# A two-layer attention and mixture-of-experts kernel: layer 0's experts computed on their chosen tokens only

## The chip, the cores and the metric

The kernel runs on one core of a Trainium2 chip. The metric is the device time of one execution in microseconds (us). Engines are named as the profile names them: PE (TensorE matmuls; PEld its weight loads), DVE (VectorE), ACT (ScalarE), POOL (GpSimd) and SP (SyncE, which only starts DMAs here). Each engine runs its own list of instructions in order, and they wait for each other by semaphores.

## The reference

`x` is 8 tiles of 128 tokens with 512 features. Four residual steps follow one another, each on a layer-normed `x`: attention 0, feed-forward 0, attention 1, feed-forward 1. Only feed-forward 0 is changed:

```
scores = sigmoid(x @ gate_w.T) + bias             # 1024 tokens, 16 experts
topk_w, topk_idx = top_k(scores, 4)
cw = one_hot(topk_idx) * topk_w / sum(topk_w)     # zero for the 12 experts not chosen
g, u = x @ Wg[e].T, x @ Wu[e].T                   # 512 -> 256, for every expert e
out  = sum_e cw[:, e] * ((silu(g) * u) @ Wd[e].T) # 256 -> 512
out += (silu(x @ Sg.T) * (x @ Su.T)) @ Sd.T       # a shared expert, for all tokens
```

## The kernel before

Every product of two matrices is made in three matmuls: each operand is split in a high part (a copy rounded to fp32r, made on ACT) and a low part (the rest, made on DVE or POOL), and `three` gives hi*hi, hi*lo and lo*hi. So each weight that arrives by DMA costs a copy and a subtraction before PE may use it.

Attention 0 ends at 279 us of the span. Then `tensor_experts`, `scalar_experts` and `vector_experts` run over 34 passes: 17 experts (the shared one is number 0), each on two halves of 512 tokens. A pass is 4 groups of 12 matmuls into the hidden layer (`tensor_hidden`, 128 hidden units by 512 tokens each) and 4 groups of 6 out of it (`tensor_output`). Every expert sees every token; `vector_output` adds the result times `cw`, which is zero for most. One expert's weights are 1.5 MB, loaded by SP (`sync_experts`, L859) into one of two buffers, and split in 6 chunks of 128x512 by ACT (L904) and DVE (L909) once per two passes. The routing (`vector_routing`, about 12 small DVE operations) lies beside matmuls of pass 1.

Attention 1 follows. Its start is `opening`: keys of the context half, the layer norm of `x` (norm group 4), keys of the latent half; then `half_steps` with values and queries. In the kernel before, this opening is woven into the last expert passes. `scalar_weight`/`vector_weight` split its weights, 256 KB each, loaded by SP at L1147.

All orders are written out by hand: each engine's list is the order of the calls in its function. POOL does nothing between 279 us and the first softmax of attention 1 (it waits at L1349).

Of the kernel before, what the change touches and what calls it, by code (L numbers as in the profile page):

```python
# [8 lines left out]
U32 = mybir.dt.uint32  # L9
ALU = mybir.AluOpType  # L10
# [3 lines left out]
P = 128  # L14
B = 8
# [13 lines left out]
CH = 512  # L29

# [114 lines left out]
def layers_kernel(nc, A, out):  # L145
    with ExitStack() as whole:
# [66 lines left out]

        place[0] = PHASE
        xnB = pair("xnB", [P, KT, HT])
        xnT = [xnA, xnB]
        s_act = [sb(f"silu{i}", [P, HT]) for i in range(2)]
        z = [sb(f"z{i}", [P, HT]) for i in range(2)]
        zs = [pair("zs0", [P, IT, HT])]
# [7 lines left out]
        cw = sb("cw", [P, B, E0])  # L227
        zs.append(pair("zs1", [P, IT, HT]))
        raw.append(sb("wf_raw1", [P, 3, 2, CH]))
        wf.append(pair("wf1", [P, 3, 2, CH]))  # L230
        above_experts = place[0]
        mx = sb("mxf", [P, B, 8])
# [14 lines left out]
        k1T = pair("k1T", [P, KV1, 2, HT])  # L247
        place[0] = w1_at = max(place[0], above_experts)
# [5 lines left out]
        outw = [pair(f"w1o{i}", [P, D]) for i in range(UH)] + outw  # L254
        mx1 = [sb(f"mx1_{i}", [P, 4 * UH]) for i in range(4)]

# [61 lines left out]

        def norm_scale(g, k):
            t, b = HB * g + k, norm_tile(g, k)  # L320
            if t >= 2:
                dve.wait_ge(S["xn_turned"], t - 1)
            nc.vector.tensor_scalar(xn[t % 2][:, :], x[:, b, :], moments[:, b, 0:1], rstd[:, b:b + 1],  # L323
                                    ALU.subtract, ALU.mult).then_inc(S["xn"], 1)

        def norm_turn(g, k, n):
# [4 lines left out]
            for c in range(KT):  # L331
                ins = nc.tensor.transpose(ps[:, c * P:(c + 1) * P], xn[t % 2][:, c * P:(c + 1) * P], ident)  # L332
# [31 lines left out]
        def sync_attention0():  # L364
# [7 lines left out]
            load(bk[:, :], A["bk0"]).then_inc(S["ld_bk0"], 16)  # L372
# [3 lines left out]
            load(bv[:, :], A["bv0"].broadcast_to([P, P])).then_inc(S["ld_bv0"], 16)  # L376
            load(w_raw[:, :, :], A["wq0"]).then_inc(S["ld_wq0"], 16)
            load(bq[:, :], A["bq0"]).then_inc(S["ld_bq0"], 16)
            load(bo[:, :], A["bo0"].broadcast_to([P, D])).then_inc(S["ld_bo0"], 16)
# [151 lines left out]
        def scalar_attention0():  # L531
            def keys(half):
                act.wait_ge(S["k0_mm"], half + 1)
                act.wait_ge(S["ld_bk0"], 16)
# [30 lines left out]
            def query(half, m):  # L565
                act.wait_ge(S["ld_bq0"], 16)
# [7 lines left out]
            def out_weight(k):  # L574
                act.wait_ge(S["ld_wo0"], 16)
                nc.scalar.activation(wo[0][:, k, :], w_raw[:, k, :], ACT.Copy).then_inc(S["wo0_hi"], 1)
# [1337 lines left out]
```

## Time and profile before

| | us |
|---|---|
| median of 3 runs | 1607.87 (1607.38 to 1609.44) |
| the profiled execution, its own time | 1609.84 |
| its span in the trace | 1608.5 |
| PE busy / DVE / ACT / POOL | 1550.5 / 932.6 / 708.3 / 298.1 |
| DMA queue of SP | 78.03 MB, 14.7% of the 16 engines' time |

PE is busy for 96% of the span. The granted clock of TensorE is 0.978 of full speed on average. The times of single matmuls overlap (each is modelled as 0.39 us long, while one starts every 0.23 us), so the pace of PE is read from starts, or from a run of matmuls divided by its count.

### The profile page before, as it was taken

Reading aid. Unit: us, or ns where it says so; the run is one execution under the profiler, and the core shown is the slowest. Engines: PE = TensorE matmul, PEld = TensorE weight load, DVE = VectorE, ACT = ScalarE, POOL = GpSimd, SP = SyncE. Lnnn points to the kernel's source line nnn. Section 1 sums busy time; section 2 is a strip of 40 time slices with the busy share of each in tenths; the row PEclk is TensorE's granted clock in tenths of the full one; section 3 lists DMA queues with packets and bytes.
Section 4 is the critical chain, followed back from the end, with each engine's and each line's share of the span. In section 5 each row is a group of like instructions: output and inputs, shape, how many; then the busy total and the mean of one; then the engine's idle time right before and its main releaser. Section 6 shows DMA issues by size and latency. Waiting matters only on the chain.

```text
span 1608.5 us, 19926 instructions
## 1 busy us (share of the span) xinstructions
PE 1550.5 (96%) x7394; PEld 1253.3 (78%) x7394; DVE 932.6 (58%) x1762; ACT 708.3 (44%) x1899; POOL 298.1 (19%) x566
## 2 busy tenths in 40 slices
PE   6989988999999999999999999999989999999997
PEld 5667655788888888888887888888877888888875
DVE  5576885545444444444545566666764566666767
ACT  3665875422222222222223455555653455555632
POOL 4354563000000000000000123223220222232200
PEclk7699999999999999999999999999999999999999
DMA  5000100211211112111011211112121121121101
GB/s 187 1 1 1 41 1 10 109 40 40 78 40 40 40 41 77 40 40 59 0 53 31 68 53 58 55 53 66 53 66 53 53 63 62 53 68 58 66 0 53
DMA packets 29666, 79.30 MB, mean 49 GB/s; under 512 B 3969, under 2 KB 4353, under 8 KB 26881
## 3 DMA queue, kind: packets, MB, share of 16 engines
q1 hardware_dynamic: 29568, 78.03, 14.7%
q8 instruction: 58, 0.95, 0.2%
q14 instruction: 40, 0.32, 0.1%
HBM read 75.92 MB, written 2.10 MB: 48 GB/s over the span
## 4 chain that ended last, share of the span: by engine, by line
PE 88%; DVE 6%; ACT 3%; POOL 1%; issue 1%; DMA 1%; SPq 0%; DVEq 0%; ACTq 0%
PE bank L352 75%; PE bank L1381 5%; PE bank L1357 3%; PE bank L490 2%; PE bank L478 2%; ACT p L587 1%; POOL p L817 1%; DVE xn L323 1%; DVE p0T_lo L723 1%; DVE k0d_hi L684 1%; PE bank L332 0%; DVE stats L304 0%; DMA ctx_raw<-in_ctxT 0%; ACT p0T_hi L596 0%; DVE xnA_lo L346 0%
## 5 line engine op out<-in xcount | busy, mean ns | idle before, releaser
L1349 POOL TENSOR_SCALAR p<-p,mx 128x256 f32<-128x256 f32 x256 | 163.8, 658 | 1104.6 <-DVE mx L1343 1104.6
L945 DVE TENSOR_TENSOR z<-bank,silu 128x512 f32<-128x512 f32 x68 | 47.0, 691 | 202.7 <-PE bank L352 201.0
L938 ACT ACTIVATE zs_hi<-z 128x512 fp32r<-128x512 f32 x68 | 43.0, 632 | 188.4 <-DVE z L945 188.4
L1335 ACT ACTIVATE p<-bank,mx 128x256 f32<-128x256 f32 x256 | 118.1, 486 | 11.3 <-DVE mx L1325 11.1
L352 PE MATMUL bank<-xnA_hi,w1q_hi 128*128 128x512 f32 x288 | 117.9, 409 | 2.2 <-DVE xnA_lo L346 1.7
L969 DVE SCALAR_TENSOR_TENSOR x<-bank,cw,x 128x512 f32<-128x512 f32 x128 | 93.8, 748 | 38.0 <-PE bank L352 38.0
L352 PE MATMUL bank<-xnA_hi,w1q_lo 128*128 128x512 f32 x288 | 114.1, 396 | 0.0
L352 PE MATMUL bank<-xnA_lo,w1q_hi 128*128 128x512 f32 x288 | 113.5, 394 | 0.0
L817 POOL TENSOR_SCALAR p<-p,sx 128x128 f32<-128x128 f32 x256 | 91.6, 379 | 113.6 <-DVE sx L711 113.4
L352 PE MATMUL bank<-wf_hi,zs_hi 128*128 128x512 f32 x272 | 108.0, 397 | 1.8 <-DVE zs_lo L948 1.8
L352 PE MATMUL bank<-wf_lo,zs_hi 128*128 128x512 f32 x272 | 107.5, 395 | 0.0
L352 PE MATMUL bank<-wf_hi,zs_lo 128*128 128x512 f32 x272 | 107.3, 394 | 0.0
L352 PE MATMUL bank<-xnA_hi,wf_lo 128*128 128x512 f32 x272 | 107.2, 394 | 0.0
L352 PE MATMUL bank<-xnA_lo,wf_hi 128*128 128x512 f32 x272 | 107.0, 393 | 0.0
L352 PE MATMUL bank<-xnA_hi,wf_hi 128*128 128x512 f32 x272 | 106.7, 392 | 0.0
L352 PE MATMUL bank<-xnB_lo,wf_hi 128*128 128x512 f32 x272 | 106.7, 392 | 0.0
L352 PE MATMUL bank<-xnB_hi,wf_lo 128*128 128x512 f32 x272 | 106.7, 392 | 0.0
L352 PE MATMUL bank<-xnB_hi,wf_hi 128*128 128x512 f32 x272 | 106.7, 392 | 0.0
L352 PE MATMUL bank<-w1o_hi,a1T_hi 128*128 128x512 f32 x256 | 105.3, 411 | 0.1
L933 ACT ACTIVATE silu<-bank 128x512 f32<-128x512 f32 x68 | 40.3, 593 | 145.1 <-PE bank L352 145.1
L1364 ACT ACTIVATE p1T_hi<-bank 128x512 fp32r<-128x512 f32 x128 | 75.2, 596 | 65.7 <-PE bank L1357 65.6
L352 PE MATMUL bank<-w1o_hi,a1T_lo 128*128 128x512 f32 x256 | 100.4, 392 | 0.0
(287 smaller groups left out, 3936.3 us busy)
## 6 DMA issues: line engine op xcount, KB each, us to landing
wf_raw<-in_wffn SPq DMA_DIRECT2D x17, 1536.0 KB, 6.6
w_raw<-in_wq SPq DMA_DIRECT2D x64, 256.0 KB, 2.7
w_raw<-in_wo SPq DMA_DIRECT2D x64, 256.0 KB, 2.7
x<-in_x SPq DMA_DIRECT2D x8, 256.0 KB, 7.3
w_raw<-in_wk SPq DMA_DIRECT2D x8, 256.0 KB, 2.9
w_raw<-in_ctxT SPq DMA_DIRECT2D x8, 256.0 KB, 3.4
w_raw<-in_wv SPq DMA_DIRECT2D x8, 256.0 KB, 2.7
out<-x SPq DMA_DIRECT2D x8, 256.0 KB, 2.1
```

The costliest lines, as they stand in the source:

```text
L352: ins = nc.tensor.matmul(ps, a, b, start=(n == 0), stop=(n == len(pairs) - 1))
L478: ins = nc.tensor.transpose(ps[:, g * P:(g + 1) * P], pr0[:, i % PR, g, :], ident)
L817: ins = nc.gpsimd.tensor_scalar(pr0[:, j, g, :], pr0[:, j, g, :], sx[:, k, 3, g:g + 1], 1.0, ALU.mult, ALU.mult)
L933: nc.scalar.activation(s_act[t % 2][:, :], banks.of(("up", n, it, 0))[:, :], ACT.Silu).then_inc(S["silu"], 1)
L938: nc.scalar.activation(zs[n % 2][0][:, it, :], z[t % 2][:, :], ACT.Copy).then_inc(S["zs_hi"], 1)
L945: nc.vector.tensor_tensor(z[t % 2][:, :], banks.of(("up", n, it, 1))[:, :], s_act[t % 2][:, :], ALU.mult).then_inc(S["z"], 1)
L969: ins = nc.vector.scalar_tensor_tensor(out=x[:, tile, :], in0=ps[:, :], scalar=cw[:, tile, e - 1:e], in1=x[:, tile, :], op0=ALU.mult, op1= ...
L1335: ins = nc.scalar.activation(pr1[s % 2][:, h, :], banks.of(("s1", s, n))[:, hh * 2 * P:(hh + 1) * 2 * P], ACT.Exp, bias=m[:, UH + h:UH + h ...
L1349: ins = nc.gpsimd.tensor_scalar(pr1[s % 2][:, h, :], pr1[s % 2][:, h, :], m[:, 3 * UH + h:3 * UH + h + 1], 1.0, ALU.mult, ALU.mult)
L1357: ins = nc.tensor.transpose(ps[:, h * P:(h + 1) * P], pr1[s % 2][:, h, part * P:(part + 1) * P], ident)
L1364: nc.scalar.activation(p1T[0][:, part, :], banks.of(("t1", s, part))[:, :], ACT.Copy).then_inc(S["p1T_hi"], 1)
L1381: ins = nc.tensor.matmul(ps[:, :], a, c, start=(part == 0 and n == 0), stop=(part == 1 and n == 2))
```

## The change

The experts are computed on the (token, expert) pairs that were chosen, 4096 in all. Each expert's pairs are given whole tiles of 128 rows; whatever the routing, 47 tiles are enough, and all 47 are run. The stage has 55 steps of 128 rows (8 of the shared expert on the tokens as they lie, then 47), numbered n; tile j is step n = 8 + j and has its own load of an expert's weights, number m = j + 1.

The new parts: the normed tokens stay in `xn8`; a DMA fills `xs_rows` (12.3 MB in HBM) with zeros; `tensor_ranks` and `vector_slots` give each pair its row and each tile its expert; POOL scatters the tokens in 32 indirect DMAs of 128 rows; SP loads the rows of each tile (`xs`, 256 KB) and its expert's weights (1.5 MB, its address from a register); PE transposes the rows, makes gate and up in one group of 12 matmuls, transposes the hidden tile, and makes the 6 matmuls out of it; ACT copies the result out of PSUM and POOL stores it (256 KB). At the end POOL gathers each token's four results in 32 indirect DMAs, and DVE adds them to `x` in `vector_return`. The low part of the down weights moves to POOL (`wd_lo`). The first opening of attention 1 comes after the experts (`first_opening`), in another order. The rest is renamed semaphores and moved buffers.

```diff
+TILES = (B * P * TOP0 + E0 * (P - 1)) // P          # 47
+FFN_STEPS = B + TILES                               # 55
 def sync_experts():
-            for e in range(E0 + 1):
-                if e == 1:
-                    sp.wait_ge(S["y0_mm"], B)
-                if e >= 2:
-                    sp.wait_ge(S["wf_lo"], 6 * (e - 1))
-                load(raw[e % 2][:, :, :, :], A["wffn"][e]).then_inc(S[f"ld_wf{e % 2}"], 16)
+            load(raw[0][:, :, :, :], A["wffn"][0]).then_inc(S["ld_wf0"], 16)
+            sp.wait_ge(S["vp_zero"], 5)
+            load(xs_rows.rearrange("(n p) d -> p n d", p=P),
+                 zeros.unsqueeze(1).broadcast_to([P, TILES, D])).then_inc(S["zero_fill"], 16)
+            def weights(m):
+                if m > TILES:
+                    return
+                if m >= 3:
+                    sp.wait_ge(S["gu_lo"], 4 * (m - 2))
+                    sp.wait_ge(S["wd_lo"], 2 * (m - 2))
+                e = nc.values_load(tile_e[0:1, m - 1:m], engines=(SP,), min_val=1, max_val=E0, ...
+                load(raw[m % 3][:, :, :, :], A["wffn"][e]).then_inc(S[f"ld_wf{m % 3}"], 16)
+            sp.wait_ge(S["routed"], 1)
+            for m in (1, 2, 3):
+                weights(m)
+            sp.wait_ge(S["scattered"], 16 * B * TOP0)
+            for j in range(TILES):
+                if j >= 4:
+                    sp.wait_ge(S["xs_turned"], j - 3)
+                load(xs[j % 4][:, :], xs_rows[j * P:(j + 1) * P, :]).then_inc(S[f"ld_xs{j % 4}"], 16)
+                weights(j + 4)
 def tensor_experts():
-            for n in range(PASSES - 2):
-                tensor_hidden(n)
...
+            for n in range(FFN_STEPS + 1):
+                if n >= 1:
+                    tensor_z_turn(n - 1)
+                if n < FFN_STEPS:
+                    tensor_gate_up(n)
+                if n in (1, 2):
+                    for k in (2 * n - 2, 2 * n - 1):
+                        norm_turn(3, k, next(turn_ring))
+                if n == 3:
+                    tensor_gate(1, next(turn_ring))
+                if n == 4:
+                    tensor_gate_turn(1, next(turn_ring))
+                if n == 5:
+                    tensor_ranks()
+                if B <= n + 1 < FFN_STEPS:
+                    tensor_x_turn(n + 1 - B)
+                if n >= 1:
+                    tensor_down(n - 1)
 def scalar_experts():
+            for n in range(FFN_STEPS + 2):
+                j = n - B
+                if 1 <= n <= FFN_STEPS:
+                    scalar_z(n - 1)
+                if n - 2 >= B:
+                    scalar_rows_out(n - 2)
+                if 0 <= j < TILES:
+                    for c in range(2):
+                        scalar_wd(j + 1, c)
+                if 0 <= j < TILES - 1:
+                    for c in range(2):
+                        scalar_gu(j + 2, c)
+                if n < FFN_STEPS:
+                    scalar_silu(n)
...
+                        scalar_x(j + 1)
+                    for c in range(2, 4):
+                        scalar_gu(j + 2, c)
 def gpsimd_experts():
+            pool.wait_ge(S["slots"], 1)
+            for b in range(B):
+                for k in range(TOP0):
+                    nc.gpsimd.indirect_dma_start(
+                        out=xs_rows, out_offset=bass.IndirectOffsetOnAxis(ap=slots[:, b, k:k + 1], axis=0),
+                        in_=xn8[:, b, :], in_offset=None).then_inc(S["scattered"], 16)
+            for j in range(TILES):
+                for c in range(2):
+                    wd_lo(pool, nc.gpsimd, j + 1, c)
+                if j >= 2:
+                    store(j - 2)
+            for j in (TILES - 2, TILES - 1):
+                store(j)
+            for i in range(Y_RING):
+                pool.wait_ge(S[f"st_ys{i}"], 16 * len(range(i, TILES, Y_RING)))
...
+                for k in range(TOP0):
+                    nc.gpsimd.indirect_dma_start(
+                        out=returned[b % RETURNS][:, k, :], out_offset=None, in_=ys_rows,
+                        in_offset=bass.IndirectOffsetOnAxis(ap=slots[:, b, k:k + 1],
+                                                            axis=0)).then_inc(S[f"returned{b % HB}"], 16)
 def first_opening(weight, keys, values, back, norm):
+            for _ in range(2 * KT):
+                weight()
+            for g in range(KV1):
+                keys(0, g)
+                weight()
+                back(g)
+            for b in range(HB):
+                values(0, b)
+                norm(4, 2 * b)
+                norm(4, 2 * b + 1) if b < 3 else None
+            for g in range(KV1):
+                keys(0, KV1 + g)
+                back(HB + g)
```

## Rows read from the trace of the kernel before

**Rows 1.** The page's sections 1 and 2: busy times, and slices of the span.
```profile
PE 1550.5 (96%) x7394; PEld 1253.3 (78%) x7394; DVE 932.6 (58%) x1762; ACT 708.3 (44%) x1899; POOL 298.1 (19%) x566
PE   6989988999999999999999999999989999999997
```

**Rows 2.** The chain that ended last in order of time: start us, us, what.
```profile
279.42 11.36 PE bank L352 x48
...
316.01 535.44 PE bank L352 x2328
```

**Rows 3.** The same chain around the end of the experts.
```profile
857.85 2.57 PE bank L352 x6
...
862.43 1.41 PE bank L352 x6
```

**Rows 4.** Timeline of PE there: start us, us, engine, line, operation, idle before it.
```profile
856.76 1.08 PE L332 MATMUL bank<-consts,xn 128*128 128x128 f32 x8 [2.60 <-DVE xn L323]
857.61 0.67 PE L352 MATMUL bank<-wf_hi,zs_hi 128*128 128x512 f32 x1
```

**Rows 5.** Windows: us, busy of PE, PEld, DVE, ACT, POOL, granted clock, DMA share, GB/s.
```profile
316.00:850.00 534.00, 534.00 (x2324) 436.44 (x2324) 246.66 (x391) 131.20 (x228) 0.00 (x0) 1.00 0.12 44
857.00:861.00 4.00, 4.00 (x18) 3.15 (x16) 2.37 (x5) 1.08 (x2) 0.00 (x0) 0.59 0.00 0
280.00:287.00 7.00, 7.00 (x32) 5.68 (x31) 3.97 (x11) 3.46 (x4) 0.00 (x0) 1.00 1.01 390
```

**Rows 6.** The page's section 6, DMA issues: count, KB each, median us to landing.
```profile
wf_raw<-in_wffn SPq DMA_DIRECT2D x17, 1536.0 KB, 6.6
w_raw<-in_wo SPq DMA_DIRECT2D x64, 256.0 KB, 2.7
out<-x SPq DMA_DIRECT2D x8, 256.0 KB, 2.1
...
w_raw<-in_wq SPq DMA_DIRECT2D x1, 1024.0 KB, 8.2
...
bq<-in_bq SPq DMA_DIRECT2D x1, 2.0 KB, 7.9
```

**Rows 7.** Timeline of SP's issues at the start: start us, us.
```profile
7.28 0.44 SPq L377 DMA_DIRECT2D w_raw<-in_wq  x1
7.76 0.45 SPq L378 DMA_DIRECT2D bq<-in_bq  x1
```

**Rows 8.** Groups by line and form on POOL: busy us, mean ns.
```profile
L831 POOL TENSOR_TENSOR wq_lo<-w_raw,wq_hi 128x512 fp32r<-128x512 f32 x4 | 5.4, 1374 | 4.5 <-ACT wq_hi L624 4.5
```

**Rows 9.** Timeline of ACT: six chunks of weights, and a copy out of PSUM with its successor.
```profile
305.31 3.22 ACT L904 ACTIVATE wf_hi<-wf_raw 128x512 fp32r<-128x512 f32 x6
308.55 1.28 ACT L933 ACT_TABLE_LOAD   x1
...
867.00 0.60 ACT L1205 ACTIVATE k1T_hi<-bank 128x512 fp32r<-128x512 f32 x1 [3.94 <-PE bank L352]
867.50 0.62 ACT L1174 ACTIVATE w1o_hi<-w_raw 128x512 fp32r<-128x512 f32 x1
```

**Rows 10.** Groups on DVE from 278 to 832 us, by form.
```profile
L969 DVE SCALAR_TENSOR_TENSOR x<-bank,cw,x 128x512 f32<-128x512 f32 x120 | 88.1, 749 | 37.3 <-PE bank L352 37.3
L909 DVE TENSOR_TENSOR wf_lo<-wf_raw,wf_hi 128x512 fp32r<-128x512 f32 x96 | 59.2, 686 | 3.5 <-ACT wf_hi L904 3.5
```

**Rows 11.** Timeline of DVE: the routing's first and largest operations, and the layer norm.
```profile
318.03 0.64 DVE L976 MAX8 mxf<-sc 128x8 f32<-128x16 f32 x7
...
320.28 0.69 DVE L982 TENSOR_TENSOR ohf<-mifl,consts 128x512 f32<-128x512 f32 x1
321.01 1.05 DVE L989 TENSOR_REDUCE cw<-ohf 128x128 f32<-128x512 f32 x1
...
285.26 0.55 DVE L323 TENSOR_SCALAR xn<-x,moments,rstd 128x512 f32<-128x512 f32 x1 [0.26 <-DVE rstd L317]
```

**Rows 12.** Timeline of PE: the first matmul of attention 1's third query.
```profile
897.22 0.40 PE L352 MATMUL bank<-xnA_hi,w1q_hi 128*128 128x512 f32 x1
```

More of the change, by code:

```diff
@@ L235, in layers_kernel @@
         oh = sb("ohf", [P, B, TOP0, E0])
-        ssum = sb("ssum", [P, B])
+        taken = sb("taken", [P, B, E0], F32R)
+        over = sb("over", [P, E0, B])
+        tiles_of = sb("tiles_of", [P, E0])
+        upto = sb("upto", [P, E0, E0])
+        ends = sb("ends", [P, E0])
+        starts = sb("starts", [P, E0])
+        slot_of_e = sb("slot_of_e", [P, B, E0])
+        slot_f = sb("slot_f", [P, B, TOP0])
+        ended = sb("ended", [P, TILES, E0])
+        tile_f = sb("tile_f", [P, TILES])
+        ssum = sb("ssum", [P, B])
+        place[0] = PHASE - 2 * D * 4
+        below = sb("below", [P, P], F32R)
+        ones_r = sb("ones_r", [P, P], F32R)
+        not_after = sb("not_after", [P, E0, E0])
+        by_p8 = sb("by_p8", [P, B])
+        by_p = sb("by_p", [P, TILES])
+        diff = sb("diff", [P, P])
+        assert place[0] <= PHASE
+        place[0] = PHASE + 16 * HT * 4
+        RETURNS = 6
+        returned = [sb(f"returned{i}", [P, TOP0, D]) for i in range(RETURNS)]
         place[0] = PHASE
@@ L951, in tensor_output @@
[L951 to L972 removed]
+        GU_CHUNKS = [(0, 0), (1, 0), (0, 1), (1, 1)]
@@ new lines, in scalar_expert_weight, with vector_expert_weight, step_tokens @@
+        def scalar_expert_weight(n):
+            if n < 4:
+                scalar_gu(0, n)
+            else:
+                scalar_wd(0, n - 4)
+        def vector_expert_weight(n):
+            if n < 4:
+                vector_gu(0, n)
+            else:
+                wd_lo(dve, nc.vector, 0, n - 4)
+        def step_tokens(n):
+            if n < B:
+                h, cols = n // HB, slice((n % HB) * P, (n % HB + 1) * P)
+                return tuple(q[:, :, cols] for q in xnT[h])
+            return tuple(q[:, :, :] for q in xsT[(n - B) % 2])
@@ new lines, in tensor_gate_up, with both @@
+        def tensor_gate_up(n):
+            m = weights_of(n)
+            ps = banks.take(next(gu_ring), ("gu", n), (S["z"], n + 1))
+            pe.wait_ge(S["gu_lo"], 4 * (m + 1))
+            if n < B:
+                pe.wait_ge(S["xn_lo"], HB * (n // HB + 3))
+            else:
+                pe.wait_ge(S["xsT_lo"], n - B + 1)
+            hi, lo = step_tokens(n)
+            w = wf[m % 2]
+            def both(part, k):
+                return w[part][:, 0:2, k // 2, (k % 2) * I0:(k % 2 + 1) * I0]
+            mm_group(ps[:, :], [q for k in range(KT) for q in three(
+                (hi[:, k, :], lo[:, k, :]), (both(0, k), both(1, k)))]).then_inc(S["gu_mm"], 1)
@@ new lines, in tensor_ranks @@
+        def tensor_ranks():
+            ps = banks.take(next(turn_ring), "ranks", (S["routed"], 1))
+            pe.wait_ge(S["taken"], 2)
+            pe.wait_ge(S["rank_consts"], 7)
+            flat = taken[:, :, :].rearrange("p b e -> p (b e)")
+            nc.tensor.matmul(ps[:, 0:B * E0], below[:, :], flat, start=True, stop=False)
+            for d in range(1, B):
+                nc.tensor.matmul(ps[:, d * E0:B * E0], ones_r[:, :], flat[:, 0:(B - d) * E0], start=False,
+                                 stop=(d == B - 1))
+            for b in range(B):
+                ins = nc.tensor.matmul(ps[:, B * E0:(B + 1) * E0], ones_r[:, :], taken[:, b, :], start=(b == 0),
+                                       stop=(b == B - 1))
+            ins.then_inc(S["ranks"], 1)
@@ new lines, in vector_return @@
+        def vector_return(b):
+            dve.wait_ge(S[f"returned{b % HB}"], 16 * TOP0 * (b // HB + 1))
+            dve.wait_ge(S["shared_add"], b + 1)
+            dve.wait_ge(S["routed"], 1)
+            for k in range(TOP0):
+                ins = nc.vector.scalar_tensor_tensor(
+                    out=x[:, b, :], in0=returned[b % RETURNS][:, k, :], scalar=share[:, b, k:k + 1],
+                    in1=x[:, b, :], op0=ALU.mult, op1=ALU.add)
+                if k < TOP0 - 1:
+                    vstep.step(ins)
+            ins.then_inc(S["moe_add"], 1)
```

551 lines of the change are left out of this document (317 added, 234 removed).

## The prediction

> **What bounds the kernel now.** I read the busy shares first, then the chain that ended last in order of time, then windows and single timelines at the two ends of the expert stage. PE is busy in 96% of the span and in 9 tenths or more of nearly every slice [rows 1], and the chain shows one piece of 2328 matmuls without a gap in 535.44 us [rows 2]: a matmul of 512 columns starts every 0.230 us. The 34 passes hold 34 x 72 = 2448 of them, 563 us, more than a third of the span, at the full granted clock and with DMA at 0.12 of its capacity [rows 5]. Nothing but PE's own work bounds the stage; ACT, DVE, POOL and DMA have room.
>
> **What is removed.** 2448 matmuls, 563 us, become 55 steps x 18 = 990, 228 us, plus 6 transposes a tile. If PE stayed the bound, a step would cost 18 x 0.230 + about 0.7 = 4.9 us and the kernel would end some 290 us earlier. So the question is what a step waits for.
>
> **What a tile costs, engine by engine.** ACT: six chunks of weights at 3.22/6 = 0.54 us, two copies of 512 columns out of PSUM at 0.50 (start to next start), two of 256 columns at some 0.3: 4.8 us [rows 9]. DVE: four subtractions at 0.6, one more, two of half size: 3.7 us (59.2 us for 96, overlapping slightly) [rows 10]. POOL: two subtractions at 1.37 us and the issue of a store: about 4 us [rows 8]. DMA: 1.57 + 0.26 + 0.26 MB at the 390 GB/s of a window with DMA share 1.01: 5.4 us [rows 5]. By throughput alone a tile would take 5.5 to 6 us, and the kernel would win.
>
> **The wait that decides.** SP's list is: rows of tile j, then weights(j+4), then rows of tile j+1. weights(m) first waits until the buffer of m - 3 has been split, that is wd_lo of weights j+1, and these are the weights of the tile being computed. So the 256 KB of rows of tile j+1, whose own four buffers are free, stand behind that wait, and also behind the 1.5 MB in the same DMA queue. PE transposes these rows in step n = 8 + j, one step later than the previous ones. This closes a loop of one tile with no slack:
> x_turn(j) on PE, down(n-2), z_turn(n-1), then ACT: z(n-1), rows out, two chunks wd(j+1), then POOL: wd_lo twice, then SP: register load, issue of the weights, issue of the rows, then both transfers, then x_turn(j+1).
>
> Its price, from the landing of rows j:
> - PE: four transposes to the next matmul 0.85 us, six matmuls 2.57, two transposes to their end about 0.7: 4.2 us with hops. These are the slow figures [rows 3, 4]. They apply because PE will have idled before each landing: in the rows, after 2.60 us of idle, the granted clock of the next stretch is 0.59 on average (between the levels 1.2 and 2.4 GHz) and six matmuls take 2.57 us, where at full clock they take 1.41. At full clock this piece is 2.3 us.
> - ACT: z 0.3, rows out 0.5, first wd chunk to its end 0.6: 1.4 us [rows 9].
> - POOL: 2 x 1.37 = 2.7 us; the second ACT chunk is hidden under the first [rows 8].
> - SP: hop 0.1, register load from SBUF. The trace has no such load. Its bounds are 0.3 (a DMA issue takes 0.44 [rows 7]) and 3 us (the landing of a 256 KB transfer, 2.7 [rows 6]); I take 0.9, nearer the issue since a few bytes are read. Together 1.0.
> - DMA: weights alone land 6.6 us after issue; the rows issued behind add 0.26 MB/390 GB/s = 0.7. Why behind: bq, 2 KB, issued 0.48 us after the 1 MB of wq [rows 7], lands 7.9 us after issue, at 15.66, and wq at 7.28 + 8.2 = 15.48 [rows 6]. The small one comes out just after the large one. With hops: 7.4.
> Sum 4.2 + 1.4 + 2.7 + 1.0 + 7.4 = 16.7 us a tile. Bounds: 14.2 (full clock, register load 0.3) and 19.5 (load 3 us, the store of another tile in the same transfer, 0.7). The gate holds for the rows of tiles 1 to 44 (weights(48) and later return at once): 44 x 16.7 = 735 us (625 to 858).
> The Trainium skill (TensorE: Matmul & The Clock Gate, section "HAM oscillation — how this bites in real kernels") describes a loop whose work per tile is shorter than its wait for data, so that each tile starts at the slow clock. By its rule the slow figures stand in all 44 turns; were the clock kept, the sum would be 44 x 1.9 = 84 us less, and the trace's one gap agrees with the rule.
>
> **Before the first tile.** The stage starts at 279.4 [rows 2]. Earlier, 48 matmuls (11.36 us) covered the norm on DVE; now the first gate-up is 12 matmuls, 2.8 us. DVE has the four statistics, `xn` until 285.8 [rows 11] and vector_choice(0) before z(0): the eight-tile version runs from 318.03 to 322.1 [rows 11], half of it some 2.5 us. PE waits until about 289, 7 us idle. Steps 1 to 5 take 5 x 4.5, the gate's 12 matmuls 2.8, the norm's transposes with their waits 4, table loads of 1.28 us [rows 9] about 2: gate-up 5 ends at 320. Sixteen short matmuls of tensor_ranks follow, 2 us. vector_slots needs eight operations until the rows are known, the widest 0.69 and 1.05 [rows 11], 4 us with their waits: 326. Now POOL scatters. Nothing in the trace is like it. Below: 256 KB at 390 GB/s, 0.67 us each. Above: one after another like a store, 0.5 to issue + 2.1 to land = 2.6 [rows 6]. I take 1.3, near POOL's own passes of 1.37 us over a tile of the same size [rows 8], since the work is POOL's: 32 x 1.3 = 42 us, landing 2, the rows of tile 0 2.7: they are there at **373** (352 to 414). PE's shared steps end near 335, so nearly all of it is on the path. The zero fill, 12.3 MB, takes 32 us at 390 GB/s, from about 185; its reader on DVE needs it at 285, so it is hidden down to a rate of 120 GB/s. The constants on POOL, the weights 1 to 3 and the memset lie in idle time of theirs.
> The Trainium skill (DMA: Bandwidth & Descriptors, section "Anatomy of one DMA — SWDGE (gpsimd) path") gives a DMA issued by GpSimd about 2.0 us fixed plus bytes/436 GB/s; strung one after another the 32 would take 83 us by that estimate, 41 more than I take. No row shows whether they overlap.
>
> **After the last tile.** Rows 44 land at 373 + 735 = 1108. The last three tiles have their rows early and run at about 5.9 us (ACT, the split of the last two chunks and gate-up in series); the last down ends 24 us later, 1132. Copy, store and its landing: 4. Then 16 gathers before the norm of group 4 can see its tiles, 16 x 1.3 + 2.7: 1160. Four additions of 0.75 [rows 10] for the last of them 3; statistics, sqrt with its table, and scale, transposes, two value groups of the context half that stand between them in PE's list, partly at the slow clock: 19, so 1182. Four groups of keys begin; on DVE each is followed by vector_return (4 x 0.75 and waits, 3.1) of tiles 4 to 7, 3.8 a turn against PE's 2.76, so DVE leads: back(7) ends near 1201 and the first query's low part at 1201.4. The third query needs it. It stood at 897.22 [rows 12]. From there the kernel is as before: 1608.5 - 897.2 = 711.3. The context keys and two value groups before (17 us) fill the wait for the gathers and cost nothing extra.
> Sum: 1201.4 + 711.3 = 1912.7 of span; + 1.3 around it = 1914; the profiled run is 2 above the median (1609.84 to 1607.87): **1912 us**.
>
> **The rivals.**
> 1. The two transfers share the engines instead of following each other: the rows land about 3.3 us after their issue. Then a turn is 4.2 + 1.4 + 2.7 + 1.0 + 0.4 + 3.3 = 13.0, 44 x 3.7 = 163 us less: 1750. For it: four DMAs can be started in 2 us; against it the 2 KB of bq. Under 10%, with other shortenings of the same size 14%.
> 2. Not slower: the rows of j+1 don't wait for the split at all (my reading of the two lists is off by one step). Then the throughput figures hold, 5.9 us a tile, 44 x 10.8 = 475 less: 1437. The point from which it decides: with all else as above, the kernel is even at (1912 - 1608)/44 = 6.9 less, 9.8 us a tile. Even sharing engines at full clock with the cheapest register load gives 2.3 + 1.4 + 2.7 + 0.4 + 0.4 + 2.7 = 9.9. 5% for clearly faster, 1% for within 0.2%.
> 3. Software DMA on POOL is dear: scatter and gather at 2.6 us each (42 + 21 more at least), and its stores and descriptors stretch POOL's subtractions and the queue to 19 us a turn (101 more): 2076. 14%.
> 4. It doesn't do what it says: it does; all 47 tiles run, filled or not, and the computed address costs one register load each. Nothing depends on the routing but which expert is read.
>
> **How the numbers follow.** Forecast 66%, rival 1 14%, rival 2 6%, rival 3 14%. Faster by over 0.2%, about the least a measurement here can tell: 0.05; within: 0.01; slower: 0.94. The forecast's own bounds are 1780 to 2040 (the loop's ends and a third of the others'). The range takes in rival 1 and half of rival 3: 1740 to 2060.
>
> **What would show it.** PE busy between about 380 and 1110 us in bursts of 8 us out of 16 to 17, granted clock well below 1 there; x_turn's transposes idle before them and released by the DMA of `xs`; SP's issue of the weights idle for DVE's or POOL's `wd_lo`, and the issue of `xs` right behind it; DMA share near a third. A gap of some 35 us on PE before tile 0 with indirect DMAs on POOL. Wrong: tiles at under 10 us, or `xs` landing long before its transposes.

## The result, and the profile after

| | before | after |
|---|---|---|
| median | 1608.65 us (4 runs) | 1905.79 us (4 runs, 1901.47 to 1907.22) |
| span of the profiled execution | 1608.5 | 1905.4 |
| PE busy / DVE / ACT / POOL | 1550.5 / 932.6 / 708.3 / 298.1 | 1365.7 / 965.4 / 814.2 / 528.5 |
| bytes on SP's queue | 78.03 MB, 14.7% | 151.43 MB, 22.4% |

The change makes the kernel slower: the time is 1.184 of that of before (interval 1.182 to 1.187). The forecast was 1912 us.

The page of after, sections 1, 2 and 4. The lines of before are [rows 1].

```profile
PE 1365.7 (72%) x6250; PEld 1084.5 (57%) x6250; DVE 965.4 (51%) x1795; ACT 814.2 (43%) x2153; POOL 528.5 (28%) x779
...
PE   6899978144444444444444556999999999999997
...
PEclk7799988677677776777777778999999999999999
...
PE 56%; DMA 17%; POOL 10%; DVE 7%; ACT 5%; issue 3%; SPq 2%; ACTq 0%; POOLq 0%
```

PE has 185 us less of busy time, and the kernel takes 297 us more. In slices 9 to 22 PE is busy 4 tenths where it was 9, and no other engine is busier than 3 tenths there. A low share on every engine at once suggests that they take turns; the chain says the same, for it now holds DMA, POOL and SP. The window of the tiles puts numbers on it (us, then busy time of PE, PEld, DVE, ACT, POOL, granted clock, DMA share, GB/s); before, the stage stood as in [rows 5].

```profile
372.00:1100.00 728.00, 327.19 (x1101) 250.79 (x1101) 236.94 (x320) 225.03 (x455) 158.56 (x136) 0.71 0.35 129
```

What a turn consists of is read from the chain of waits of after, over one tile (start us, us, what; short pieces of issue left out):

```profile
686.79 6.82 DMA xs<-xs_rows
...
693.65 1.11 PE bank L1100 x4
694.76 2.56 PE bank L403 x6
697.32 0.44 PE bank L1056 x2
...
698.07 0.59 ACT ys L1093
698.66 0.53 ACT wf_hi L996
...
699.27 2.98 POOL wf_lo L1000 x2
...
702.32 0.27 SPq L924
...
702.76 0.33 SPq L926
...
703.15 6.60 DMA xs<-xs_rows
...
709.79 1.12 PE bank L1100 x4
```

It is the predicted loop, piece by piece: rows land, PE turns them (L1100), makes the down product of the tile before (L403) and turns the hidden tile (L1056), ACT copies z, the result and the first down chunk, POOL makes both remainders (L1000), SP reads the expert's number (L924), issues the weights (L926) and the rows behind them, and the rows land 6.60 us later. The list of SP's waits names the gate (engine line <- releaser: us in total, times, longest):

```profile
SPq L79 <- POOL wf_lo L1000: 650.7, 44, 15.6
```

44 times, for tiles 1 to 44. And the landing times (page, section 6: count, KB, median us), where before had the weights alone at 6.6 [rows 6]:

```profile
wf_raw<-in_wffn SPq DMA_DIRECT2D x48, 1536.0 KB, 6.6
...
xs<-xs_rows SPq DMA_DIRECT2D x47, 256.0 KB, 6.8
```

### The profile page after: what moved, and what is told of

Same layout as the page of the kernel before. It is cut to its first block, busy times and chain, and to the rows that moved or that the text cites. A ratio compares the mean times of both kernels' runs of the same rounds, so it can differ in the third digit from the quotient of the medians.

```text
span 1905.4 us, 18405 instructions
## 1 busy us (share of the span) xinstructions
PE 1365.7 (72%) x6250; PEld 1084.5 (57%) x6250; DVE 965.4 (51%) x1795; ACT 814.2 (43%) x2153; POOL 528.5 (28%) x779
## 3 DMA queue, kind: packets, MB, share of 16 engines
q1 hardware_dynamic: 46832, 151.43, 22.4%
## 4 chain that ended last, share of the span: by engine, by line
PE 56%; DMA 17%; POOL 10%; DVE 7%; ACT 5%; issue 3%; SPq 2%; ACTq 0%; POOLq 0%
PE bank L403 40%; DMA xs<-xs_rows 16%; POOL wf_lo L1000 7%; PE bank L1658 5%; PE bank L1100 3%; PE bank L1634 3%; PE bank L541 2%; PE bank L529 2%; POOL xs_rows L1296 2%; ACT ys L1093 1%; ACT wf_hi L996 1%; PE bank L1056 1%; SPq L926 1%; DVE x L1331 1%; POOL p L868 1%
## 5 line engine op out<-in xcount | busy, mean ns | idle before, releaser
L1100 PE MATMUL bank<-consts,xs 128*128 128x128 f32 x188 | 51.3, 427 | 434.2 <-DMA xs<-xs_rows 434.2
L1000 POOL TENSOR_TENSOR wf_lo<-wf_raw,wf_hi 128x512 fp32r<-128x512 f32 x94 | 138.9, 1495 | 579.9 <-ACT wf_hi L996 579.9
L1100 PEld LDWEIGHTS bank<-consts,xs 128*128 128x128 f32 x188 | 33.2, 214 | 453.5 <-DMA xs<-xs_rows 407.8
L989 DVE TENSOR_TENSOR wf_lo<-wf_raw,wf_hi 128x512 fp32r<-128x512 f32 x192 | 180.5, 979 | 72.8 <-ACT wf_hi L984 72.8
L403 PE MATMUL bank<-xnA_hi,w1q_hi 128*128 128x512 f32 x288 | 118.6, 412 | 11.3 <-DVE w1q_lo L1446 8.0
L403 PE MATMUL bank<-xnA_hi,w1q_lo 128*128 128x512 f32 x288 | 114.6, 398 | 0.0
L403 PE MATMUL bank<-xnA_lo,w1q_hi 128*128 128x512 f32 x288 | 113.9, 396 | 0.0
L984 ACT ACTIVATE wf_hi<-wf_raw 128x512 fp32r<-128x512 f32 x192 | 110.0, 626 | 0.9 <-DMA wf_raw<-in_wffn 0.9
L403 PE MATMUL bank<-w1o_hi,a1T_hi 128*128 128x512 f32 x256 | 105.2, 411 | 0.1
L403 PE MATMUL bank<-w1o_hi,a1T_lo 128*128 128x512 f32 x256 | 100.3, 392 | 0.0
L403 PE MATMUL bank<-w1o_lo,a1T_hi 128*128 128x512 f32 x256 | 100.1, 391 | 0.0
L1566 ACT ACTIVATE q1T_hi<-bank 128x512 fp32r<-128x512 f32 x64 | 38.3, 598 | 132.3 <-PE bank L403 132.3
L403 PE MATMUL bank<-wf_hi,xsT_hi 128*128 128x512 f32 x188 | 90.3, 481 | 3.1 <-DVE wf_lo L989 2.9
L1572 DVE TENSOR_TENSOR q1T_lo<-bank,q1T_hi 128x512 fp32r<-128x512 f32 x64 | 44.2, 691 | 94.5 <-ACT q1T_hi L1566 94.5
L638 ACT ACTIVATE p<-bank,sx 128x128 f32<-128x128 f32 x256 | 91.0, 383 | 1.5 <-DVE sx L769 1.5
L1646 DVE TENSOR_TENSOR p1T_lo<-bank,p1T_hi 128x512 fp32r<-128x512 f32 x128 | 86.2, 681 | 0.0
## 6 DMA issues: line engine op xcount, KB each, us to landing
xs_rows<-xn SPq DMA_DIRECT2D x1, 12032.0 KB, 33.3
```

What stands on the lines that cost most here:

```text
L403: ins = nc.tensor.matmul(ps, a, b, start=(n == 0), stop=(n == len(pairs) - 1))
L638: ins = nc.scalar.activation(pr0[:, j, g, :], ps[:, g * P:(g + 1) * P], ACT.Exp, bias=sx[:, k, 1, g:g + 1], scale=SCALE0, accum_out=sx[:, ...
L984: nc.scalar.activation(wf[m % 2][0][:, a, c, :], raw[m % 3][:, a, c, :], ACT.Copy).then_inc(S["gu_hi"], 1)
L989: nc.vector.tensor_tensor(wf[m % 2][1][:, a, c, :], raw[m % 3][:, a, c, :], wf[m % 2][0][:, a, c, :].bitcast(F32), ALU.subtract).then_inc( ...
L1000: engine.tensor_tensor(wf[m % 2][1][:, 2, c, :], raw[m % 3][:, 2, c, :], wf[m % 2][0][:, 2, c, :].bitcast(F32), ALU.subtract).then_inc(S[" ...
L1100: ins = nc.tensor.transpose(ps[:, k * P:(k + 1) * P], xs[j % 4][:, k * P:(k + 1) * P], ident)
```

## The experiments

The first three experiments (e1 to e3) take the loop apart and e4 tries a small term of it. e5, e6, e10 and e11 ask what binds once it is gone, and e7 to e9 work on the two ends of the stage. The theory and its rivals stand in each expectation. A time without a range beside it is that of one run.

**The rows ahead of the weights' wait (e1_rows_ahead).** Only SP's order changes; all work stays.

```diff
-            for j in range(TILES):
+            def rows(j):
+                if j >= TILES:
+                    return
                 if j >= 4:
                     sp.wait_ge(S["xs_turned"], j - 3)
                 load(xs[j % 4][:, :], xs_rows[j * P:(j + 1) * P, :]).then_inc(S[f"ld_xs{j % 4}"], 16)
+            for j in range(3):
+                rows(j)
+            for j in range(TILES):
+                rows(j + 3)
                 weights(j + 4)
```

> The changed kernel, with one edit in SP's list: the rows of tile j+3 are issued ahead of the weights j+4, where the changed kernel issued the rows of j+1 behind them; four row buffers allow it. Theory (the loop through SP's list sets 16.24 us a tile): the rows are there long before their transposes, and a tile takes what the last tiles of the changed kernel take, about 7.5 us from gate-up to gate-up (1095.23 to 1102.70), at least 6.8 by DVE's list beside POOL; 44 x 8.8 = 387 us less than 1906, so about 1519 (1485 to 1550), faster than before. PE's wait for xs nearly gone. Rival 1 (the 1.5 MB of weights a tile, their buffers and landing of 6.6 us set the pace): 13 us or more a tile, over 1750. Rival 2 (POOL's two subtractions and store, 3.6 us of POOL, hold the loop by themselves): over 10 us a tile, above 1630.

Measured: 1459.39 us (1454.66 to 1464.17), 0.909 of before (interval 0.905 to 0.914), below the expected band of 1485 to 1550. PE waits for the DMA of `xs` once, before the first tile. The window 400 to 600 us:

```profile
400.00:600.00 200.00, 165.13 (x783) 129.26 (x782) 163.38 (x228) 159.91 (x325) 113.23 (x98) 1.00 0.92 340
```

From 389.74 to 642.35 us (two issues of weights on SP) 41 tiles pass, 6.16 us each, where the expectation had 7.5. So the loop is the whole of the loss and more: without it the change is worth 9%. The granted clock is 1.00 (2.4 GHz) over the window and no longer 0.71. My 7.5 us was taken from the free last tiles of after (gate-ups start at 1095.23 and 1102.70), where the first gate-up runs at the slower clock behind a gap: 4.26 us (1095.23 to 1099.49, granted clock 0.64), in the next tile 2.86 (1.00). With the clock back a tile costs less.

**The rows between the wait and the weights (e2_rows_before_weights).** The gate stays (the rows wait for the split), but they are issued ahead of the register load and of the 1.5 MB.

```diff
+                if j + 4 <= TILES:
+                    sp.wait_ge(S["gu_lo"], 4 * (j + 2))
+                    sp.wait_ge(S["wd_lo"], 2 * (j + 2))
+                rows(j + 1)
                 weights(j + 4)
```

(Cut: `rows` is the function of e1, and the same two waits are taken out of `weights`.)

> The changed kernel, with the rows of tile j+1 issued after the same wait for the split of weights j+1, but ahead of the register load and of the 1.5 MB. It parts the two things the rows stood behind. Theory (transfers of one queue leave in order, so the rows waited 4.2 us of the 6.9 for the weights' bytes): the rows land 2.7 us after the wait's release plus issue; the turn loses 4.2 + 0.8 = 5.0 us: 11.2 a tile, about 1685 (1660 to 1710). Rival (transfers in one queue share the engines, order of issue means nothing): only the 0.8 us of register load and issue are gained, 15.4 a tile, about 1870. If the wait itself costs little and the queue everything, the tile falls to 7.5, about 1520.

Measured: 1689.23 us, within the expected band. The chain of waits:

```profile
706.17 1.11 PE bank L1106 x4
...
711.79 2.97 POOL wf_lo L1006 x2
...
714.81 3.09 DMA xs<-xs_rows
...
717.95 0.66 PE bank L1106 x4
```

The rows land 3.09 us after the wait ends instead of 6.60 behind the weights, and with SP's work on the weights gone from the loop too this turn takes 11.78 us, in after 16.14. From the first turn of rows to the last (365.0 to 881.4) it is 516.4 us, in after 730.6 (369.2 to 1099.8). So the loss has two halves: of the 446 us between after and e1, 217 come from standing behind the transfer and its issue (4 of them lie before the first tile). The rest, 230, is what the gate itself costs: while it stands, the split and the rows' own landing of 3.1 us are part of every turn. The gated turns take 11.43 us on average (365.00 to 867.72, 44 of them), 4.81 less than in after. The medians of the landing (3.1 against 6.8) and SP's work on the weights (0.90 us in after's turn, 702.25 to 703.15, against 0.05) give 4.55 of these. The prediction put break-even at 9.8 us a tile; at this turn the kernel is still slower than before.

**The down weights' remainder back on DVE (e3_down_split_on_dve).**

```diff
 def vector_experts():
...
+                if 0 <= j < TILES:
+                    for c in range(2):
+                        wd_lo(dve, nc.vector, j + 1, c)
...
 def gpsimd_experts():
...
-                for c in range(2):
-                    wd_lo(pool, nc.gpsimd, j + 1, c)
```

> The changed kernel, with the low part of the down weights made on DVE instead of POOL, at the place in DVE's list where ACT has just made the high part. SP's list unchanged. Theory (POOL's 2.98 us are a term of the loop): from the end of the first high part the loop needs 0.54 + 0.65 = 1.2 us instead of 3.0, so 14.4 us a tile, about 1827 (1810 to 1845); DVE's own four chunks fall from 0.99 to about 0.65 us each, which is off the loop. Rival (POOL's work is hidden and weights set the pace): no change, 1900 to 1912.

Measured: 1815.88 us, within the expected band. In the chain POOL's 2.98 us became

```profile
715.03 1.30 DVE wf_lo L1000 x2
...
717.24 6.60 DMA xs<-xs_rows
```

and this turn 14.41 us. The span fell by 91.0 us (1905.4 to 1814.4). 44 x (2.98 - 1.30) = 74 of them are the replaced term. From the first turn of rows to the last it is 643.4 us (364.9 to 1008.3), 87 less than in after: 13 more than the term gives. 10 of these lie in the 44 gated turns (14.33 us on average, in after 16.24), and a landing of the rows that is 0.2 us shorter by the medians (6.6 against 6.8) gives 9. The other 3 lie in the last two tiles, where a gate-up runs at the slow clock in after and at the fast one here (4.26 us from 1095.23 against 2.85 from 1005.11). The last 4 of the 91 stand before the first tile, where the two kernels are the same. The transfer is untouched, so POOL's speed is one term of the loop and no cause of its own.

**A fixed address (e4_fixed_address).** The expert is a constant of the tile and no longer computed; the experts used are then not those that the routing chose, so that part of the computation is changed, while each engine's work stays.

```diff
-                e = nc.values_load(tile_e[0:1, m - 1:m], engines=(SP,), min_val=1, max_val=E0, ...)
+                e = 1 + (m - 1) % E0
```

> The changed kernel, with the weights loaded from addresses fixed when the program is built (expert 1 + j mod 16 for tile j): the register load is left out, and the wrong expert's weights are used for most rows. Theory (the chain shows 0.27 us at the register load and about 0.2 us of register work before the issue): 0.3 to 0.5 us a tile, 44 times: about 1888 (1880 to 1896). Rival (a computed address makes the transfer itself slower, by the addressing or by descriptors): landing under 6 us and over 30 us less in all.

Measured: 1901.57 us; expected were 1880 to 1896. The register load is gone from the chain, but

```profile
712.15 0.33 SPq L925
...
712.52 7.20 DMA xs<-xs_rows
```

the rows land 7.20 us after their issue, 0.60 later than in after's turn shown (by the medians 7.2 against 6.8), and this eats the gain; the weights land later too (median 7.1 against 6.6). 44 turns took 711.1 us (364.99 to 1076.10), 3.6 less than in after. SP's part of a turn fell from 0.90 us to 0.44 (712.08 to 712.52), so 44 x 0.46 = 20 were to go, and the later landing takes about 44 x 0.4 = 18 back. Nothing else changed in the loop. A possible reason is that here each tile reads another expert than the tile before, while in after neighbouring tiles often read the same one; it wasn't tried, and stays open. What follows is only that taking the computed address away gains no more than a few us of 1900.

**Both repairs (e5_ahead_and_dve).** e1 and e3 together.

> Both earlier edits together: rows issued three tiles ahead, and the low part of the down weights on DVE. With the rows ahead alone a tile took 6.15 us at DMA share 0.90 to 0.92 and PE waited for DVE's wf_lo. Theory A (the loop is now gate-up, transposes of x, ACT's x and last two chunks, DVE's last chunk, next gate-up: 2.8 + 0.4 + 0.2 + 0.6 + 1.15 + 0.65 = 5.8, with DVE's chunks at 0.65 us once POOL is quiet): 5.8 us a tile, 44 x 0.35 = 15 us less, about 1444 (1435 to 1452). Theory B (the transfers bind: 6.15 x 0.92 = 5.65 at share 1.0): the same size, with DMA share at 0.97 or above. Rival (POOL's share of the work mattered, DVE is now the bound): 6.2 or more, no gain.

Measured: 1453.17 us (1452.25 to 1454.9), 0.905 of before (0.904 to 0.907), a little above the expected band. A tile takes 6.08 us. Its chain of waits no longer holds a transfer:

```profile
501.26 0.69 DVE xsT_lo L1120
501.95 1.21 DVE wf_lo L996 x2
...
503.20 3.02 PE bank L403 x12
506.22 0.45 PE bank L1107 x4
...
506.69 0.61 ACT xsT_hi L1115
```

PE turns the rows of the next tile only after the gate-up group, ACT and DVE split them, then DVE splits the last two gate-up chunks, and only then PE may go on: 3.02 + 0.45 + 0.61 + 0.69 + 1.21 and hops = 6.08. DVE's part of this is about what it was in e1 (0.60 + 1.21 us there, 0.69 + 1.21 here): the work that it took over from POOL stands at another place of its list.

**A third of the bytes (e6_third_of_bytes).** As e5, but from the fourth tile on only the down weights are loaded; gate and up weights of earlier tiles are used again, so that part of the computation is changed. The DMA share of e5 was 0.95 in the same window; does it bind?

```diff
-                load(raw[m % 3][:, :, :, :], A["wffn"][e]).then_inc(S[f"ld_wf{m % 3}"], 16)
+                if m < 4:
+                    load(raw[m % 3][:, :, :, :], A["wffn"][e]).then_inc(S[f"ld_wf{m % 3}"], 16)
+                else:
+                    load(raw[m % 3][:, 2, :, :], A["wffn"][e][:, 2, :, :]).then_inc(S[f"ld_wf{m % 3}"], 16)
```

> As the kernel with both edits, but from the fourth expert tile on only the down weights are loaded (0.5 MB of 1.5): the gate and up weights stay those of an earlier tile, everything else runs as before. Theory A (the chain of PE, ACT and DVE sets the pace): less than 0.15 us a tile, within 8 us of the kernel with both edits, and DMA share about 0.45. Theory B (the transfers set it): the tile falls to the chain's 5.3 to 5.6, 15 us or more less.

Measured: 1455.19 us and 6.083 us a tile, the same as e5, at

```profile
400.00:600.00 200.00, 167.41 (x792) 130.77 (x791) 169.06 (x297) 162.37 (x330) 17.76 (x33) 1.00 0.53 173
```

Half the DMA share and not a microsecond gained: a share of 0.95 on its own is no proof of a bound.

**The routing earlier (e7_routing_two_steps_earlier).** As e5, with the norm's transposes one or two steps of the stage earlier, and gate, choice, ranks and slots two steps, in all lists, for example:

```diff
-                if n == 3:
+                if n == 1:
                     tensor_gate(1, next(turn_ring))
-                if n == 5:
+                if n == 3:
                     tensor_ranks()
```

> As the kernel with both edits, but the norm of the second half, the gate, the choice and the slots stand two steps earlier in all lists. Theory (PE stands still for 36 us before the first tile because 32 scatters at 1.27 us each follow the slots; the shared steps hide none of it that they could not hide earlier): the scatters start two steps, 8 to 10 us, earlier and the first tile's transposes too; PE waits as much as it did less nothing, the whole kernel ends 7 to 10 us earlier. Rival (the end of the shared steps or the norm's chain on DVE sets the start): under 3 us.

Measured: 1443.04 us; its span is 11.8 below that of e5, where 7 to 10 were expected. PE's wait before the first tile (timeline of PE; e5 had 36.66 us, until 365.03):

```profile
353.66 1.09 PE L1107 MATMUL bank<-consts,xs 128*128 128x128 f32 x4 [29.28 <-DMA xs<-xs_rows]
```

The tile starts 11.4 us earlier, and no other part moves: what stands before the scatters is on the path one for one, and the scatters themselves (40 us) still are.

**The opening's weights earlier (e8_opening_weights_earlier).** As e5, but the eight chunks of weights and context with which attention 1 opens are split in the last four steps of the experts.

```diff
 def scalar_experts():
+                if FFN_STEPS - 3 <= n <= FFN_STEPS:
+                    scalar_weight()
+                    scalar_weight()
 def first_opening(weight, keys, values, back, norm):
-            for _ in range(2 * KT):
-                weight()
```

(`vector_experts` alike.)

> As the kernel with both edits, but the eight chunks of weights and context for the opening of attention 1 are split on ACT and DVE in the last four steps of the experts, two a step, instead of after them. Theory (in the changed kernel PE stood 13.69 us for these before the first keys, but behind them the gathers of the first four tiles land at about 27 us after the last store, so only part comes back): PE's wait before the first keys falls under 4 us, and the kernel ends 5 to 8 us earlier. Rival 1 (the norm waits for this chain alone): 13 us earlier. Rival 2 (the gathers alone): 0 to 2.

Measured: 1451.85 us; 2.9 us of span, where 5 to 8 were expected. PE's wait before the context keys fell from 14.27 to 2.46 us, but (timelines of PE and of DVE):

```profile
687.72 0.77 PE L403 MATMUL bank<-w1o_hi,q1T_hi 128*128 128x512 f32 x1 [14.56 <-DVE w1o_lo L1460]
```
```profile
672.28 3.11 DVE L1345 SCALAR_TENSOR_TENSOR x<-returned,share,x 128x512 f32<-128x512 f32 x4 [5.31 <-DMA returned<-ys_rows,slots]
```

the wait moved to the values (6.60 in e5), behind DVE, and DVE now waits for POOL's gathers. From the last down product to the norm's transposes it is 42.5 us (656.58 to 699.10), in e5 47.0 (654.74 to 701.70): 4.4 us gained there. 1.3 of them are lost in the tiles (from the first turn of rows to the last down product 291.0 us against 289.7), where ACT and DVE now have the extra chunks, and 0.6 ahead of them. The gathers are next behind.

**All four (e9_all).** e5, e7 and e8 together.

> The whole of the repairs together: rows of the next tiles issued ahead of the weights, the down weights' remainder on DVE, the routing two steps earlier, the opening's weight chunks in the last steps of the experts. Theory A (the gains lie at different places of the chain, so they add): 1453.2 (first two) - 11.8 (routing) - 2.9 (opening) = 1438.5 us, range 1434 to 1446, time per tile 6.08 us as in each of them. Rival (earlier routing and earlier chunks share a wait at the opening, so that only the larger one counts): 1441 to 1443.

Measured: 1444.75 us (1437.72 to 1451.45), 0.901 of before (0.896 to 0.905). By its time this is no better than e7 alone; I had expected 1438.5 (1434 to 1446). Stretch by stretch the gains do add: from the last down product to the norm's transposes it takes 43.7 us (649.58 to 693.23), in e7 48.9 (643.31 to 692.25). But the first tile starts 4.2 us later than in e7 (357.86 against 353.66), although the two kernels are the same up to there, and the tiles take 2.1 us more, as in e8 (291.7 against 289.7); 2.7 of the 4.2 stand already at the first scores of attention 0 (51.00 against 48.31). The stretch before the first tile thus moves by some 4 us from run to run (it ends at 369.17 in after and at 365.0 in e2 to e5), and e9's own four runs lie 14 us apart: gains of 3 us are read from stretches, not from the times of single runs.

**All gate-up chunks first (e10_gate_up_chunks_first).** As e9, with the last two chunks moved ahead of silu and of the rows' split, out of the chain that e5 showed.

```diff
                 if 0 <= j < TILES - 1:
-                    for c in range(2):
+                    for c in range(4):
                         scalar_gu(j + 2, c)
                 if n < FFN_STEPS:
                     scalar_silu(n)
...
                         scalar_x(j + 1)
-                    for c in range(2, 4):
-                        scalar_gu(j + 2, c)
```

> As e9_all, but ACT and DVE split all four gate-up chunks of the next tile's weights before they turn to silu and to the tokens' rows, so that the chain of a tile is gate-up 3.03 + turn 0.45 + copy 0.61 + remainder 0.69 + hops 0.3 = 5.1 us and no longer 6.07. Theory A (the transfers stand right behind: 0.96 of their share at 344 GB/s with 6.08 us a tile): the tile falls only to 6.08 x 0.96 = 5.84 us, share 0.99 or more, so 41 x 0.24 = 10 us off e9_all: 1429 us, range 1424 to 1435. Rival B (the lists of ACT and DVE, 5.4 us of busy time each, bind only a little above that and the transfers can go faster): 5.5 to 5.6 us a tile, 1415 to 1420. Rival C (silu now waits behind two more chunks on ACT and the chain grows): no gain, 6.1 to 6.4 us a tile, 1439 to 1452.

Measured: 1438.4 us (1434.43 to 1445.56), 0.896 of before (0.893 to 0.899): the fastest of all, though its interval overlaps that of e9. From the first turn of rows to the last it is 277.0 us (360.0 to 637.0), in e9 281.6: 0.1 us a tile. None of the three forecasts of the expectation fits: Theory A had 0.24, Rival B more, Rival C a loss. The chain of waits took another way round:

```profile
507.34 0.45 PE bank L1063 x2
...
508.10 0.59 ACT ys L1100
508.69 0.53 ACT wf_hi L1003
...
509.24 1.29 DVE wf_lo L1007 x2
510.53 1.34 DVE wf_lo L996 x3
...
512.26 0.69 DVE wf_lo L996
512.94 0.35 DVE z L1056
```

Six chunks on DVE stand between z(n-1) and z(n), which feeds the turn of z, ACT and DVE again: 5.99 us.

**The same with a third of the bytes (e11_first_third_of_bytes).** The edit of e6 on e10; again that part of the computation is changed.

> As e10_gate_up_chunks_first, with only the down weights loaded from the fourth tile on: the gate and up weights of two thirds of the bytes stay those of earlier tiles, so part of the computation changes; instruction counts on all engines are the same. Theory A (transfers bind in e10): the tile falls further, to the 5.4 us of busy time of DVE plus little, 5.4 to 5.6 us, 41 x 0.35 = 14 us below e10. Rival B (engines' lists bind in e10): the same time as e10 within 2 us.

Measured: 1437.57 us, and 277.1 us from the first turn to the last (356.8 to 633.9): the same as e10, at a DMA share of 0.53 against 0.97. Theory A (the transfers bind) is wrong at 0.97 too; rival B stands: the lists of ACT and DVE bind. That it is their order, by the cycle in e10's chain, is read from the trace; no edit took that cycle apart.

## Why the prediction was right, and where it was off

The mechanism was the one forecast. The sum came out 7 us high, 1912.7 against 1905.4 of span, by its own terms:

| | predicted | measured |
|---|---|---|
| until rows 0 are turned | 373 | 369.2 |
| 44 turns | 735 (16.7 each) | 714.7 (16.24 each) |
| to the end of the last down product | 24 | 26.0 |
| from there to the third query (1194.53) | 69.4 | 84.6 |
| the rest | 711.3 | 710.9 |

That the sum is so close is in part luck: the turns came out 20 us shorter than worked out and the stretch behind the last tile 15 longer, and the two cancel.

**The turn.** PE 4.2 was 4.11, ACT 1.4 was 1.40. The slow figures were right to take [rows 3, 4]: four transposes took 1.11 us and six matmuls 2.56. In e2, where PE waits less, 23 of the 44 gated turns still have transposes of 1.11 or 1.12, the others shorter ones, down to 0.63. In e1 PE idles little, the clock is 1.00, and twelve matmuls take 3.01. The rule named in the prediction (the Trainium skill, TensorE: Matmul & The Clock Gate, "HAM oscillation — how this bites in real kernels") fits the rows of after: a loop that waits for data in each turn starts each turn at the slow clock, the transposes of all 44 gated turns taking 1.09 to 1.12 us. e2 shows that with a shorter wait only about half of the turns do. POOL was 2.98 and not 2.7: it took 2.96 us for two chunks beside DVE and 2.54 with DVE idle (last section), and the 1.37 of [rows 8] lies between. SP and the transfer were 7.5 together and not 8.4: the register load takes 0.27 with some 0.16 of register work behind it, where I took 0.9 between bounds of 0.3 and 3, and the rows land 6.60 after their issue, a little sooner than the weights' 6.6 plus 0.7 behind their issue. The reading of bq [rows 6, 7], a small transfer that comes out behind a large one in the same queue, carried this term, and e2 shows it: 3.09 us in front, 6.60 behind. Rival 1 (shared engines) is wrong by that.

**Before the first tile.** The timeline of POOL and that of PE:

```profile
324.20 1.23 POOL L1296 DMA_INDIRECT xs_rows<-xn,slots  x1 [52.11 <-DVE slots L1173]
...
363.85 0.96 POOL L1296 DMA_INDIRECT xs_rows<-xn,slots  x1 [0.30 <-issue]
```
```profile
369.17 1.08 PE L1100 MATMUL bank<-consts,xs 128*128 128x128 f32 x4 [36.28 <-DMA xs<-xs_rows]
```

31 intervals from 324.20 to 363.85 are 1.28 us each; I took 1.3, between 0.67 and 2.6. They start 2 us sooner than worked out. The last has landed 2.67 us after its start and the next load is issued then. The 83 us that the estimate from the Trainium skill gave (DMA: Bandwidth & Descriptors, "Anatomy of one DMA — SWDGE (gpsimd) path") would hold only if each scatter waited for the one before; here they overlap, the pace is that of POOL's issue, and rival 3 is wrong for that reason. The zero fill took 33.3 us from 185.26 on, hidden as said.

**After the last tile: the term that was wrong.** I wrote that the context keys and two value groups "fill the wait for the gathers and cost nothing extra". The timeline of PE:

```profile
1108.28 0.47 PE L403 MATMUL bank<-wf_hi,zT_hi 128*128 128x512 f32 x1 [0.98 <-ACT ys L1093]
...
1123.57 0.77 PE L403 MATMUL bank<-q1T_hi,w1q_hi 128*128 128x512 f32 x1 [13.69 <-DVE q1T_lo L1446]
...
1143.81 0.77 PE L403 MATMUL bank<-w1o_hi,q1T_hi 128*128 128x512 f32 x1 [6.55 <-DVE w1o_lo L1446]
...
1187.53 0.79 PE L403 MATMUL bank<-xnA_hi,w1q_hi 128*128 128x512 f32 x1 [7.53 <-DVE w1q_lo L1446]
```

PE does nothing for 13.69 us, since the keys need eight chunks loaded and split first, and no list does that before the last tile is through. The keys, the values and the norm come late: the keys of the latent half begin 58.7 us after the last down product (1109.9 to 1168.60), where I had 50 (1132 to 1182): 8.7 us. The timeline of DVE shows why, and what comes behind:

```profile
1129.70 0.69 DVE L1475 TENSOR_TENSOR k1T_lo<-bank,k1T_hi 128x512 fp32r<-128x512 f32 x1 [6.28 <-ACT k1T_hi L1469]
...
1143.58 3.10 DVE L1331 SCALAR_TENSOR_TENSOR x<-returned,share,x 128x512 f32<-128x512 f32 x4
...
1183.77 3.10 DVE L1331 SCALAR_TENSOR_TENSOR x<-returned,share,x 128x512 f32<-128x512 f32 x4
1186.79 1.89 DVE L1446 TENSOR_TENSOR w1q_lo<-w_raw,w1q_hi 128x512 fp32r<-128x512 f32 x3
```

The additions of the returned rows stand behind the first keys in DVE's list. None of them waits for a gather here, and the fourth tile's end at 1146.68, 36.8 us after the last down product, where I had 31. The last tile's end 18.3 us after the start of the latent keys, near the 19 that I had. But the split of the first query's weights stands behind them, so the first query waits 7.53 us, until 1187.53, and the third starts 7.0 us later; I had let the third start as soon as DVE was through. That makes 25.9 us and not 19.4. I costed matmuls and gathers and left out the splitting of the weights that the old order had hidden beside expert passes: 8.7 + 6.5 = 15.2 us. e8 tried the first part: with the eight chunks out of the way that stretch is 4.4 us shorter and no more, the gathers being next, so about half of the 8.7 is shown to be the chunks'. The other half and the second part weren't tried.

**The lists of throughput.** Rival 2's 5.9 us a tile, by throughput alone, came close once the loop is gone: e1 ran at 6.16 us a tile and ended at 1459, where that rival said 1437; e10, with the other repairs, ran at 6.02 and ended at 1438. No engine's sum of work is that long (in the window of e10 PE is busy 0.88 of the time, DVE 0.84, ACT 0.80), and the transfers don't bind (e11); what is left is the order of the lists, as the chains of e5 and e10 read. The price of the loop was read from before's trace within 3% (16.7 against 16.24).

## What to carry to other kernels

When several kinds of loads share one in-order issue list, look for the one whose wait is about the tile being computed now: everything queued behind it inherits that wait, and a load with four free buffers may have none of the slack that its buffers suggest. Issue the small load that is needed soonest ahead of both the wait and the large transfer (446 us here, by the order of SP's list alone). And a high DMA share is by itself no proof that transfers bind; take bytes away and look.

## What the runs showed of the hardware

- Two engines subtracting at once slow each other. In after (timelines of DVE and POOL, two chunks of 128x512 a line):

```profile
712.18 1.28 DVE L989 TENSOR_TENSOR wf_lo<-wf_raw,wf_hi 128x512 fp32r<-128x512 f32 x2
715.84 2.52 DVE L989 TENSOR_TENSOR wf_lo<-wf_raw,wf_hi 128x512 fp32r<-128x512 f32 x2 [1.62 <-ACT wf_hi L984]
```
```profile
714.86 2.96 POOL L1000 TENSOR_TENSOR wf_lo<-wf_raw,wf_hi 128x512 fp32r<-128x512 f32 x2 [12.12 <-ACT wf_hi L996]
...
1103.22 2.54 POOL L1000 TENSOR_TENSOR wf_lo<-wf_raw,wf_hi 128x512 fp32r<-128x512 f32 x2 [4.37 <-ACT wf_hi L996]
```

  DVE's pair at 715.84 falls on POOL's, that at 712.18 doesn't; POOL's pair at 1103.22 has an idle DVE beside it. So beside each other DVE loses 0.6 us a chunk (0.64 to 1.26) and POOL 0.2 (1.27 to 1.48). In e3, where POOL subtracts nothing, the mean on DVE is 683 ns, in after 979.
- An indirect DMA of 128 rows of 2 KB costs POOL 0.96 us and 0.30 to the next, whether it scatters or gathers (ten of the 32 gathers in after took 1.04 to 1.38); the data move beside that, for the median scatter lands 4.9 us after its issue and the next starts after 1.28.
- Behind 1.5 MB in the same queue 256 KB land 6.60 us after issue (after), ahead of them 3.09 (e2).
- A register load from SBUF takes SP 0.27 us (L924 in after's chain), and some 0.16 us pass before the issue behind it starts.
- TensorE's clock is a cost of waiting: 0.71 granted in after with a gap in each turn (372 to 1100 us), 1.00 in e1 (400 to 600 us), whose matmuls are the same ones.
- 351 GB/s at a share of 0.97 (window 400 to 600 us of e10) bound nothing: the tiles took as long as at 0.53 (e11).
